# Attention over 128 heads on one core: six instead of eight scores per head multiplied after the exponential, and each head's result copied out of PSUM by ScalarE instead of VectorE

## The reference

```python
q = (x @ Wq.T).reshape(d, n, h)        # d = 128, n = 3327, h = 8
k = (x @ Wk.T).reshape(d, n, h)
v = (x @ Wv.T).reshape(d, n, h)
a = jnp.einsum('dnh,dmh->dnm', q, k) * scale
a = a + spatial_encoding + edge_encoding      # both are adj
a = jax.nn.softmax(a, axis=2)
out = jnp.einsum('dnm,dmh->dnh', a, v)
```

## Time and profile before

| | us |
|---|---|
| median of three runs | 10890.68 |
| lowest, highest | 10887.95, 10892.81 |
| the profiled execution, its own time | 10890.68 |
| its span in the trace | 10889.0 |
| TensorE's granted clock, mean | 0.991 |

### The profile page before, as it was taken

The page is one execution under the profiler, slowest core; times in us unless marked ns, Lnnn a source line. Parts: engine busy times, 40 slices in busy tenths (PEclk is TensorE's granted clock), DMA queues, the critical chain, the costliest instruction groups (busy, mean ns, idle before and its releaser), DMA issues. The chain is left out here.

```text
span 10889.0 us, 547322 instructions
## 1 busy us (share of the span) xinstructions
PE 10540.8 (97%) x216535; PEld 6769.1 (62%) x216535; DVE 9711.5 (89%) x10382; ACT 10278.7 (94%) x9250; POOL 8479.5 (78%) x4260
## 2 busy tenths in 40 slices
PE   8749999999999999999999999999999999999998
PEld 6616666666666666666666666666666666666666
DVE  7688999999998999999998999999998999999997
ACT  4359999999999999999999999999999999999996
POOL 4347888888887888888887888888887888888885
PEclk9889999999999999999999999999999999999999
DMA  6582111111112111111112111111112111111113
GB/s 227 173 268 60 42 42 42 42 42 42 42 42 81 42 42 42 42 42 42 42 42 81 42 42 42 42 42 42 42 42 81 42 42 42 42 42 42 42 42 84
DMA packets 579450, 652.53 MB, mean 60 GB/s; under 512 B 172173, under 2 KB 517907, under 8 KB 573523
## 3 DMA queue, kind: packets, MB, share of 16 engines
q1 hardware_dynamic: 576786, 621.07, 20.6%
q0 software_dynamic: 832, 1.71, 0.0%
HBM read 485.17 MB, written 137.18 MB: 57 GB/s over the span
## 5 line engine op out<-in xcount | busy, mean ns | idle before, releaser
L1083 DVE SCALAR_TENSOR_TENSOR at_double<-attention_adj_t,at_score 128x832 f32<-128x832 f32 x9216 | 8938.5, 1016 | 916.7 <-PE at_score L1019 894.5
L999 POOL TENSOR_TENSOR at_single<-at_single,attention_adj_t 128x832 f32<-128x832 f32 x4096 | 8143.1, 1988 | 1823.6 <-ACT at_single L1100 1787.2
L1103 ACT ACTIVATE at_double<-at_double 128x1664 f32<-128x1664 f32 x4608 | 7907.3, 1743 | 15.1 <-DVE at_double L1083 14.8
L1019 PE MATMUL at_score<-at_q,at_k 128*32 128x512 bf16 (+1 forms) x106496 | 7248.4, 349 | 97.4 <-DMA at_v<-v_scratch 53.6
L1019 PEld LDWEIGHTS at_score<-at_q,at_k 128*32 128x32 bf16 x106496 | 3606.8, 145 | 2388.6 <-ACT at_single L1100 871.7
L1035 PE MATMUL at_acc<-at_double,at_v 128*9 128x208 f32 x73728 | 4845.1, 339 | 0.7 <-ACT at_double L1103 0.6
L1100 ACT ACTIVATE at_single<-at_score 128x832 f32<-128x832 f32 x4096 | 4127.6, 1008 | 40.0 <-PE at_score L1019 40.0
L1035 PEld LDWEIGHTS at_acc<-at_double,at_v 128*9 128x9 f32 x73728 | 1870.8, 91 | 898.8 <-issue 2.5
L1035 PE MATMUL at_acc<-at_single,at_v 128*9 128x208 f32 x32768 | 2152.3, 339 | 3.3 <-POOL at_single L999 2.8
L1035 PEld LDWEIGHTS at_acc<-at_single,at_v 128*9 128x9 f32 x32768 | 832.0, 91 | 406.3 <-POOL at_single L999 4.3
L287 POOL TENSOR_TENSOR layer_col_acc<-layer_col_acc,st_a_rows 128x3328 f32<-128x3328 f32 x26 | 189.2, 7278 | 181.9 <-DMA st_a_rows<-in_adj_dram 167.8
(11 more groups left out here) (123 smaller groups left out, 1363.2 us busy)
## 6 DMA issues: line engine op xcount, KB each, us to landing
at_k<-k_parts_scratch SPq DMA_DIRECT2D x1536, 156.0 KB
at_q<-q_parts_scratch SPq DMA_DIRECT2D x4608, 13.0 KB
at_v<-v_scratch SPq DMA_DIRECT2D x512, 112.5 KB
adj_t_scratch<-st_a_t SPq DMA_DIRECT2D x26, 1664.0 KB, 7.6
st_a_rows<-in_adj_dram SPq DMA_DIRECT2D x25, 1663.5 KB, 9.4
attended_scratch<-at_o SPq DMA_DIRECT2D x1920, 7.3 KB
attention_adj_t<-adj_t_scratch SPq DMA_DIRECT2D x12, 2080.0 KB, 13.9
q_parts_scratch<-pr_partsq SPq DMA_DIRECT2D x39, 512.0 KB, 4.6
```

The costliest lines, as they stand in the source:

```text
L999: pool.tensor_tensor(slot(n), slot(n), at[:, plan.chunk[n], :], ALU.mult).then_inc(multiplied, 1)
L1019: last = pe.matmul(score[plan.buffer(n)][32 * t:32 * (t + 1), a:b], keys[:, 32 * t:32 * (t + 1)], q[k][:, a:b], start=True, stop=True, til ...
L1083: dve.scalar_tensor_tensor(out=slot(n), in0=at[:, plan.chunk[n], :], scalar=2.0, in1=score[plan.buffer(n)][:, 0:NB], op0=ALU.mult, op1=ALU ...
L1103: act.activation(doubles[buffer][:], doubles[buffer][:], ACT.Exp).then_inc(exped, 1)
```

## The change

Six steps of a head are singles instead of eight, and twenty, in ten doubles, go through VectorE. There are eight buffers for doubles and four for singles. The scores run 8 steps ahead of the values instead of 9. `keep_head` moves from VectorE to ScalarE, where it stands behind the fifth unit of the next head (`KEEP_LAG` = 5), as an activation with the function Copy. The counts that go with it are one lower or higher by one: `kept` starts at 2, and `stored` at one round of stores.

```diff
-DOUBLES = 6
-SINGLES = 8
+DOUBLES = 8
+SINGLES = 4
-PRODUCTS = 8
+PRODUCTS = 6
...
-        SCORE_LEAD = 9
-        KEEP_AFTER = 12
+        SCORE_LEAD = 8
+        KEEP_LAG = 5
...
-                def keep_head(i, b, head):
-                    k = head % 2
-                    dve.wait_ge(used, STEPS * i + (b * BODIES * STEPS + (head + 1) * C + AHEAD))
-                    dve.wait_ge(stored[k], STORES * (GROUP // 2) * i + STORES * (b * BODIES * (GROUP // 2) + head // 2 + 2))
-                    dve.tensor_copy(o[k][:], acc[k][:, 0:QW]).then_inc(kept, 1)
...
-                            if n % C == KEEP_AFTER:
-                                keep_head(i, b, n // C - 1)
-                keep_head(0, BLOCKS, -1)
...
+            def keep_head(i, head):
+                act.wait_ge(used, STEPS * i + ((head + 1) * C + AHEAD))
+                act.wait_ge(stored[head % 2], STORES * (GROUP // 2) * i + STORES * (head // 2 + 1))
+                act.activation(o[head % 2][:], acc[head % 2][:, 0:QW], ACT.Copy).then_inc(kept, 1)
...
-                for m in range(1, UNITS + 1):
+                for m in range(KEEP_LAG, UNITS + KEEP_LAG):
                     if m < UNITS or more:
                         exponential(i, m)
+                    if m % (UNITS // GROUP) == KEEP_LAG - 1:
+                        keep_head(i, m // (UNITS // GROUP) - 1)
```

More of the change, by code:

```diff
@@ L958, in _ @@
                 for k in range(2):
-                    sp.sem_inc(stored[k], 2 * STORES)
+                    sp.sem_inc(stored[k], STORES)
                 sp.wait_ge(prefetched, 16 * len(Steps(PRODUCTS).prefetched))
@@ L983, in _ @@
                 for k in range(2):
-                    sp.wait_ge(stored[k], STORES * (BLOCKS * HEADS // 2 + 2))
+                    sp.wait_ge(stored[k], STORES * (BLOCKS * HEADS // 2 + 1))
         @block.gpsimd
@@ L1066, in _ @@
                     dve.memset(k_all[k][SHIFT_ROW:SHIFT_ROW + PARTS, 0:N], 1.0).then_inc(cleared, 1)
-                def keep_head(i, b, head):
-                    k = head % 2
-                    dve.wait_ge(used, STEPS * i + (b * BODIES * STEPS + (head + 1) * C + AHEAD))
-                    dve.wait_ge(stored[k], STORES * (GROUP // 2) * i + STORES * (b * BODIES * (GROUP // 2) + head // 2 + 2))
-                    dve.tensor_copy(o[k][:], acc[k][:, 0:QW]).then_inc(kept, 1)
-                dve.sem_inc(kept, 1)
                 for b in range(BLOCKS):
@@ L1103, in exponential @@
                     act.activation(doubles[buffer][:], doubles[buffer][:], ACT.Exp).then_inc(exped, 1)
+            def keep_head(i, head):
+                act.wait_ge(used, STEPS * i + ((head + 1) * C + AHEAD))
+                act.wait_ge(stored[head % 2], STORES * (GROUP // 2) * i + STORES * (head // 2 + 1))
+                act.activation(o[head % 2][:], acc[head % 2][:, 0:QW], ACT.Copy).then_inc(kept, 1)
             def body(i, more):
-                for m in range(1, UNITS + 1):
+                for m in range(KEEP_LAG, UNITS + KEEP_LAG):
                     if m < UNITS or more:
                         exponential(i, m)
+                    if m % (UNITS // GROUP) == KEEP_LAG - 1:
+                        keep_head(i, m // (UNITS // GROUP) - 1)
             with runs(act):
-                exponential(0, 0)
+                act.sem_inc(kept, 2)
+                for m in range(KEEP_LAG):
+                    exponential(0, m)
                 with act.Fori(0, BLOCKS * BODIES - 1) as i:
```

## The result

The changed kernel takes 11015.12 us (11013.76 to 11016.69) against 10891.74 us before: 1.0113 times as long, 95% interval 1.0101 to 1.0127. The forecast was 11,002 us, slower, within 10,935 to 11,185.

What follows compares the result with a forecast made beforehand. ScalarE, never idle, was taken to bound the kernel. To 10890.7 us came 512 x (-0.05 + 0.26) = +107 for the heads and +4 at the blocks: 11,002 us, range 10,935 to 11,185.

Steps and rivals of the forecast that it cites:

- The bound: In the attention ScalarE, busy for all 2000 of 2000 us, sets the pace at 19.34 us a head.
- Two singles for a double: ScalarE passes over as many elements with one instruction less in a head: -0.05 us a head.
- The copy: One 128x208 copy a head on the never idle ScalarE, hidden by nothing: 0.26 us, between 0.18 and 0.36.
- The 256-column row less its columns: A 256-column exponential on ScalarE, 0.28 us from start to start, taken as 0.24 with 48 columns less.
- The copy's wait: ScalarE's copy waiting for PE's last value of the head was to cost nothing.
- The 2 us of room: ScalarE was to reach the copy about 2 us after the last value it waits for.
- VectorE: Loses a copy, gets two more additions: 19.0 us a head, under 19.5, so off the path; cost 0.
- the two just-in-time doubles: Doubles at two places a head, ready 3.43 us after a single's end, where ScalarE arrives just in time.
- The sign I gave for this rival: ScalarE showing idle time before its doubles would mean that VectorE had become the bound.
- the 0.1 us kept for late doubles: Upper end for ScalarE waiting on VectorE: 0.05 us at each of two places in a head; 0 was taken.
- Blocks and `stream_adjacency`: Changes of block: +4 us, between 0 and 14. `stream_adjacency`: 26 exponentials fewer, hidden behind PE, 0, lower end -7.
- VectorE as the bound: Rival: VectorE's waits stay on top of its additions, 20.7 us a head, +690 us, about 11,580; chance 0.06.

Runs made afterwards that it cites:

- e4: The changed kernel with ScalarE copying each head's result twice, first into a tile that nothing reads: 11133.9 us.
- e7: The changed kernel with ScalarE's copy two units earlier (`KEEP_LAG` = 3 instead of 5): 11270.8 us.
- e3: The changed kernel with ScalarE's copy one unit earlier (`KEEP_LAG` = 4 instead of 5): 10995.2 us.
- half of the change: The kernel before with the new numbers of singles, doubles, buffers and lead, the copy staying on VectorE: 11109.6 us.

## Why the prediction was right

- *The bound.* ScalarE was it and stayed it. The head is its throughput: from end to end a single takes 0.753, a double 1.48 and the copy 0.233 us. 6 x 0.753 + 6 x 1.482 + 4 x 1.478 + 0.233 = 19.56 us, before 8 x 0.753 + 8 x 1.482 + 1.478 = 19.36.
- *Two singles for a double.* Priced at -0.05, measured 19.555 - 0.233 - 19.358 = -0.04 us a head.
- *The copy.* Priced at 0.26, measured 0.233. The 256-column row less its columns (0.24) was the best guide; the 0.02 added for two semaphores was not there. The Trainium skill ("ScalarE: Activation LUTs", What ACT_TABLE_LOAD costs) gave 0.27 us for a copy as an estimate, 0.03 to 0.04 more than the trace.
- *The copy's wait.* None, but for 1.4 us at the very end of the attention, and by e4 a second copy costs the same. The 2 us of room were about right: in e7 it stands two doubles (2.96 us) earlier and is 0.5 us too early, which leaves about 2.5.
- *VectorE.* The step was nearly wrong, and that it held is in part luck. I gave it 0.5 us a head to spare (19.0 of 19.5). An addition costs 0.935 us and not 0.95, 18.7 a head, but its two stops of 0.4 us, which the sum left out, belong to its cycle, so it needs 19.44 of 19.56: 0.1 us. That it stayed behind ScalarE hangs on the copy having left it. I said that those stops would go with the neighbouring doubles; four of six went, two stayed, at the two just-in-time doubles. The sign I gave for this rival, idle time in front of a double, did show once in four heads, 0.06 us long.
- *Unforeseen.* The long first head of each loop body, 0.05 us a head on average, about 24 us (e3 gets 20 of them back). It fell within the 0.1 us kept for late doubles, but its cause, the buffer wrap, wasn't seen. Sum of terms: 512 x (-0.036 + 0.233 + 0.046) = 124, where 107 were forecast: the copy was put 14 us too high, which made up for part of the stall.
- *Blocks and `stream_adjacency`.* About +2 against +4 for the blocks. For `stream_adjacency` 0 was forecast; the attention began 2.9 us sooner, which is no more than it varies among the experiments, so the runs don't tell it from 0.

The rival that came closest was VectorE as the bound. It was given 0.06 and didn't happen here, but with half of the change it did, at +218 us.

## What to carry to other kernels

A small instruction cost its full pass, 0.233 us for 208 columns, on an engine that never idles. Take it there only if the engine that it leaves is the tighter one, and find that out by its whole cycle, stops included: the sum of its instructions said 0.5 us to spare where there was 0.1. Two edits that each shift work between the same two engines are to be priced together, for each can be a loss alone. And when a ring of buffers is unrolled, look at the wrap: steps that aren't a multiple of the buffers left a place with less room in every round, which cost nothing here until VectorE had 20 additions.

## What the runs showed of the hardware

The record of a ScalarE instruction grows along a dense row: the same single is recorded with 0.86 us soon after a stop (5076.42) and with 1.05 us at the end of a dense row, while both end 0.753 us after the instruction before them. So its start can stand up to 0.2 us ahead of where the engine gets to it. A late start costs nothing as long as that lead isn't used up: in the kernel before two doubles start 1.54 us apart and end 1.48 apart. In the long head of the changed kernel the start is 0.28 us late and 0.17 us are lost. This is also why distances between starts, by place, make a long head look longer than distances between ends do.
